# The first stage of a token tower layer rebuilt: other engine orders, split fp32r products, normed rows on ScalarE, a joined row table, gate weights formed later

## The reference, cut to what matters

```python
h = concat(token_table[x], concat(op, var, const, struct, special)[x])     # 128 + 128 columns
# attention, linear, 16 heads of 16, per row of 128 tokens
q, k, v = layernorm(h) @ W_qkv + b_qkv
pq, pk = elu(q) + 1, elu(k) + 1
h = h + pq @ (pk^T v) / (pq . sum(pk) + 1e-6)
# FFN: each token weighs 16 experts
x2 = layernorm(h)
logits = l2norm(x2) @ l2norm(sim) - sigmoid(gates)
rw = softmax over the experts with logits > 0 (the top two, if none is)
q, k, v = sum_e rw_e * (x2 @ {q,k,v}_proj[e]);  causal softmax attention
h = h + sum_e rw_e * (attn @ o_proj[e])
```

## Time and profile before

| | |
|---|---|
| median of 3 runs | 1186.64 us (1185.41 to 1187.48) |
| the profiled execution, own time | 1176.88 us |
| its span, first to last instruction | 1175.0 us |
| busy in the span: PE, DVE, POOL, ACT | 1029.2, 928.9, 754.4, 533.6 us |
| mean granted TensorE clock | 0.973 |

### The profile page before, as it was taken

The page is one execution under the profiler, slowest core; times in us unless marked ns, Lnnn a source line. Parts: engine busy times, 40 slices in busy tenths (PEclk is TensorE's granted clock), DMA queues, the critical chain, the costliest instruction groups (busy, mean ns, idle before and its releaser), DMA issues.

```text
span 1175.0 us, 26735 instructions
## 1 busy us (share of the span) xinstructions
PE 1029.2 (88%) x6571; PEld 862.2 (73%) x6572; DVE 928.9 (79%) x3134; ACT 533.6 (45%) x1455; POOL 754.4 (64%) x975
## 2 busy tenths in 40 slices
PE   1999999999999993599999959999999999999898
PEld 0565656565666662588988849999999889988897
DVE  3789999999999996245544528999888888888898
ACT  3544444444433431234443425555555555555554
POOL 6657777777777756700000037888888888888785
PEclk9999999999999995799999979999999999999999
DMA  5642333333222225576777752333333333333230
GB/s 141 201 151 88 100 104 99 104 95 100 77 86 86 80 75 197 180 231 221 239 223 232 224 177 77 95 91 91 90 90 89 89 89 89 89 89 89 85 93 32
DMA packets 108096, 143.28 MB, mean 122 GB/s; under 512 B 15388, under 2 KB 95330, under 8 KB 107876
## 3 DMA queue, kind: packets, MB, share of 16 engines
q1 hardware_dynamic: 88004, 91.17, 24.4%
q0 software_dynamic: 18880, 50.36, 15.0%
q10 hardware_dynamic: 1152, 1.05, 0.3%
HBM read 77.37 MB, written 72.46 MB: 128 GB/s over the span
## 4 chain that ended last, share of the span: by engine, by line
PE 40%; DVE 22%; POOL 18%; issue 13%; ACT 3%; DMA 2%; POOLq 1%; SPq 0%; DVEq 0%; ACTq 0%
PE bank L1366 8%; PE bank L1291 7%; PE bank L1293 7%; PE bank L1292 7%; PE bank L1298 5%; POOL row_y L747 5%; POOL qk_neg L732 2%; POOL x2T L732 2%; PE bank L1364 2%; DVE phi L1055 2%; POOL x2T L728 2%; POOL x2T L734 2%; POOL qk_neg L728 2%; DVE h L1075 1%; POOL sorted_x L674 1%
## 5 line engine op out<-in xcount | busy, mean ns | idle before, releaser
L1291 PE MATMUL bank<-wo_hi,split_lo 128*128 128x256 f32 x1024 | 302.8, 296 | 4.6 <-DVE qk_e L1228 2.2
L1292 PE MATMUL bank<-wo_lo,split_hi 128*128 128x256 f32 x1024 | 287.3, 281 | 0.0
L1293 PE MATMUL bank<-wo_hi,split_hi 128*128 128x256 f32 x1024 | 287.2, 280 | 0.0
L1291 PEld LDWEIGHTS bank<-wo_hi,split_lo 128*128 128x128 f32 x1024 | 194.5, 190 | 9.3 <-DVE qk_e L1228 4.6
L1366 PE MATMUL bank<-w_attn,x1T 128*128 128x512 f32 (+1 forms) x512 | 201.2, 516 | 0.0
L1292 PEld LDWEIGHTS bank<-wo_lo,split_hi 128*128 128x128 f32 x1024 | 194.5, 190 | 0.0
L1293 PEld LDWEIGHTS bank<-wo_hi,split_hi 128*128 128x128 f32 x1024 | 194.0, 189 | 0.0
L843 ACT ACTIVATE h<-bank,rwo 128x256 f32<-128x256 f32 x256 | 107.4, 471 | 126.8 <-PE bank L1293 99.5
L747 POOL DMA_INDIRECT row_y<-sorted_y,pair_now x128 | 128.4, 1003 | 36.3 <-issue 28.5
L1166 DVE TENSOR_TENSOR split_lo<-bank,split_hi 128x256 fp32r<-128x256 f32 x144 | 61.2, 425 | 104.2 <-ACT split_hi L812 103.0
L740 POOL COPY pair_now<-pair_at 128x2 uint32 (+1 forms) x64 | 13.1, 205 | 195.7 <-SPq L531 195.6
(11 more groups left out here) (223 smaller groups left out, 2516.0 us busy)
## 6 DMA issues: line engine op xcount, KB each, us to landing
sorted_y<-row_y SPq DMA_DIRECT2D x36, 384.0 KB, 3.1
sorted_y<-w_attn SPq DMA_DIRECT2D x36, 384.0 KB, 3.2
row_x<-sorted_x SPq DMA_DIRECT2D x72, 128.0 KB, 2.4
h_rows<-h SPq DMA_DIRECT2D x64, 128.0 KB, 1.8
row_x<-h_rows SPq DMA_DIRECT2D x64, 128.0 KB, 2.9
out_h<-row_x SPq DMA_DIRECT2D x64, 128.0 KB, 2.0
category_table<-in_L_tok_special_table SPq DMA_DIRECT2D x10, 623.0 KB, 5.0
phi<-sorted_x SPq DMA_DIRECT2D x36, 128.0 KB, 2.1
```

The costliest lines, as they stand in the source:

```text
L1291: pe.matmul(ps, left[1][c], right[0][c], start=(c == 0), stop=False)
L1292: pe.matmul(ps, left[0][c], right[1][c], start=False, stop=False)
L1293: last = pe.matmul(ps, left[0][c], right[0][c], start=False, stop=(c == n - 1))
```

## The change: what it does

- **Products.** q, k, v of stage 1 are no longer two fp32 instructions for each half of the contraction but three fp32r ones (hi and lo parts of x1T and of W_qkv). ACT copies x1T to its hi part, DVE subtracts to get the lo part (`x1_lo`, new, every tile). W_qkv is split once, before step 1, into the space of `wo`.
- **Normed rows.** x1 and x2 move from DVE to ACT, as `activation(Identity, scale=root, bias=center)`. DVE makes the new `centers` (-mean times root), one small instruction a step.
- **Roots.** `var_inv` goes; roots_in is two instructions that don't wait for each other. Two small multiplications a group (`energy`) take its place.
- **Gates.** In stage 1 only choosing, counting and placing stay; `weights_formed` goes, and with it the parts of the others that served it. The last 8 tiles are in groups of two. Weights are formed for all 64 tiles in stage 2: a chain of nine small instructions before it, five wide ones (128x1024) in its steps 0 to 4.
- **Joined table.** `embed_table` holds token and category row side by side (1 KB pitch). SP copies both tables into it, ten pieces each of 1250 and 1246 rows of 512 bytes, one of each a step from step -4. From tile 14 on POOL gathers a tile with one indirect DMA, not two.
- **Weights.** Two a step before step 0, and the 16 pieces of `wo` are loaded and split in steps -8 to 7 of stage 2.
- **Orders.** Each engine's order in a step is new. Scatters come as soon as a group is placed; step 1 ends at step 66.

```diff
-    WHOLE_FROM = 14
+    JOINED_FROM = 14
-    GROUPS = B // QUAD
+    GROUPS = [(t, QUAD) for t in range(0, B - 8, QUAD)] + [(t, 2) for t in range(B - 8, B, 2)]
-    N_X2, N_RAW = 11, 4
-    SCATTER_LAG = 7
+    N_X2, N_RAW = 9, 4
+    LAST_STEP = B + 2
...
+        def o_weight_at(i):
+            return 3 * E + i.c + 8 if i.j is None and -8 <= i.c < 8 else None
...   # SP, step 1
+                if 0 <= i.c - COPY_FROM < COPIES:
+                    for skip, at, src in ((N_SMALL, HALF, special_table), (0, 0, token_table)):
+                        n = -(-src.shape[0] // COPIES)
+                        lo, hi = n * (i.c - COPY_FROM), min(n * (i.c - COPY_FROM + 1), src.shape[0])
+                        sp.dma_start(embed[skip + lo:skip + hi, at:at + HALF], src[lo:hi, :]).then_inc(rows_joined, 16)
...   # ACT, step 1, after qk_neg and qk_e of tile i+3
+                    act.activation(x1[:, :], h[t % 8], ACT.Identity, scale=roots[:, t, 0:1],
+                                   bias=centers[:, t, 0:1]).then_inc(done["x1_normed"], 1)
...   # then x2 of tile i+1 in the same way, x1T hi (i+4), pqT (i+3), x2T (i+1), vx (i+3), a weight
...   # DVE, step 1, in order
+   centers(row i+4); phi(i+3); den(i+2); bn_stats of h (i+6); zden(i+2)
+                if x1_tile.inside(B):
+                    after(dve, "x1_T", x1_tile)
+                    dve.tensor_tensor(x1T_s[1], ps_x1[:, 0:C], x1T_s[0].bitcast(F32), ALU.subtract
+                                      ).then_inc(done["x1_lo"], 1)
+   attn, h2, its moments (i+2); roots_in; the gate pieces; kvm(i+3), which waits for kv; a weight
...   # PE, step 1, in order
+   rank product; sums(i+2); turn x1(i+4); logits(i); turn phi(i+3); turn x2(i+1);
+   q and k (i+4), which wait for phi(i+3) and x1_lo(i+4); kv(i+3); v(i+4)
+                for c in range(CH):
+                    for x, w, end in ((1, 0, False), (0, 1, False), (0, 0, c == CH - 1)):
+                        last = pe.matmul(ps[:, 0:hi - lo], turned[x][c], w_attn_s[w][:, c, lo:hi], start=False,
+                                         stop=end)
...   # stage 2: SP, at the head of a step; ACT and DVE, at its end
+                    if o_weight_at(i) is not None:
+                        load_weight(sp, o_weight_at(i))
```

More of the change, by code:

```diff
@@ L408, in run1 @@
         def run1(eng, step):
-            for c in range(-7, B + SCATTER_LAG):
+            for c in range(-7, LAST_STEP + 1):
                 step(Tile(c))
@@ L775, in step1 @@
                     after(act, "qk_negative", tile)
+                    after(act, "phi", tile.shift(-1))
                     act.activation(qk_e[:, :], qk_neg[:, :], ACT.Exp, scale=-1.0).then_inc(done["qk_exp"], 1)
@@ L819, in step2 @@
                                  ).then_inc(done["pair_copied"], 1)
+                    if o_weight_at(i) is not None:
+                        weight_hi(act, o_weight_at(i))
                 run2(act, step2)
             def dense_way():
+                act.wait_ge(weights_v, 2)
+                act.activation(gates_shifted, gates_shifted, ACT.Exp).then_inc(weights_a, 1)
+                for e in range(E):
+                    weight_hi(act, 3 * E + e)
                 def token_tile(t, first):
@@ L1211, in _ @@
             branch(dve, sorted_way, dense_way)
+            dve.wait_ge(routed, 1)
             def add_slot(tile, s):
@@ L1326, in step1 @@
                 if tile.inside(B):
-                    after(pe, "x1_T", tile.shift(-1))
+                    after(pe, "x1_lo", tile.shift(-1))
                     after(pe, "x1_normed", tile)
                     turn(ps_x1, *halves(x1)).then_inc(done["x1_turned"], 1)
+                if i.inside(B):
+                    g = group_of(i.c)
+                    t = i.c - GROUPS[g][0]
+                    if t == 0:
+                        quad_done(pe, "gate_scaled", g - 1)
+                    after(pe, "x2_T", i)
+                    if i.c == 0:
+                        pe.wait_ge(setup_v, 7)
+                    for c in range(CH):
+                        last = pe.matmul(ps_logits[g % 2][:, t, :], halves(x2T)[c], simn[:, c, :],
+                                         start=(c == 0), stop=(c == CH - 1))
+                    last.then_inc(done["logits_product"], 1)
+                tile = i.shift(3)
+                if tile.inside(B):
+                    after(pe, "phi_q_T", tile.shift(-1))
+                    after(pe, "phi", tile)
+                    turn(ps_pq, *halves(phi)).then_inc(done["phi_q_turned"], 1)
                 tile = i.shift(1)
@@ L1334, in step1 @@
                     turn(ps_x2, *halves(x2[tile.c % N_X2])).then_inc(done["x2_turned"], 1)
+                tile = i.shift(4)
+                if tile.inside(B):
+                    after(pe, "phi", tile.shift(-1))
+                    after(pe, "x1_lo", tile)
+                    if tile.c == 0:
+                        pe.wait_ge(setup_v, 6)
+                    attn_product(tile, ps_qk, 0, 2 * C, "qk_product")
                 tile = i.shift(3)
@@ L1337, in step1 @@
                     after(pe, "v_copied", tile)
-                    after(pe, "phi_q_T", tile.shift(-1))
                     after(pe, "kv_masked", tile.shift(-1))
-                    after(pe, "phi", tile)
-                    turn(ps_pq, *halves(phi)).then_inc(done["phi_q_turned"], 1)
                     for g in range(G):
```

507 lines of the change are left out of this document (281 added, 226 removed).

## The result

The changed kernel takes 1202.42 us (median of four runs, 1197.76 to 1205.23) where the kernel before takes 1186.26 beside it: ratio 1.0132, 95% interval 1.0097 to 1.0166. It is slower by 1.3%, where the prediction said 1150 us and faster. Some 12 of them are there because the profiled execution of before is 9.4 us faster than its median and that of the changed kernel 2.8 slower.

A forecast was written before the change was run, and what follows sets the result against it. DVE's instruction chain was taken to bound steps with weights, a PE-ACT-DVE ring those without. Steady steps -50.6, joined table +10, way to stage 2 -5, stage 2's start +9: -36.6, span 1138.4, median 1150 us; range 1122 to 1178.

The forecast's parts named there:

- The joined table: Steps -1 to 5: the 512-byte copies make seven steps 8.0 us instead of 6.5, +10 us.
- Rival (1): Early steps: 512-byte packets cost far more than 30 ns; from 55 ns they eat all the gain; chance 0.08.
- Steady steps: Stage 1, tiles 10 to 63: 5.69 us a step with weights, 5.40 without, gain 50.6 us.
- 5.0 a step: Stage 1: PE's work falls from 6.06 to 5.0 us a step, under DVE's.
- 7 x 0.24: Stage 1, PE: q and k products of a tile take 1.68 us, for 2.33 before.
- the ring that the prediction drew: Stage 1's light step with weights: phi to x1_lo, q and k, kv, kvm, weight split, centers, 4.9 to 5.0 us.
- Rival (3): Stage 1: the new order makes longer waits, each step 6.0 us, 24 us more, 1174; chance 0.13.
- The rival that took the figure of the Trainium skill: Stage 1: ACT copies x1T 0.2 us late each step, 11 us in 53 steps, 1161; chance 0.12.
- x1_lo without wait: Stage 1, DVE: a sign expected in the trace, x1_lo starting without waiting; no size given.
- The way to stage 2: Last q and k product to stage 2's first turn: 37.3 us for 42.2, gain 5.
- about 23: Before stage 2: the fills begin about 23 us after the last product, for 25.6 before.
- Stage 2's start: First sorted tiles: tile 0 is 4 us late and steps 0 to 7 add 5, together +9 us.

The follow-up runs named there:

- later or spread o weights: Changed kernel with o weights loaded and split in steps 8 to 23 of stage 2, 1200.2 us; or loaded every second step, split six steps later, 1197.2 us.
- even copies: Changed kernel with table copies of 1264 and 1248 rows nine times, and what is left the tenth time: 1204.1 us, ratio 1.0234.
- three-edits run: Changed kernel with tables apart again, gathers a step sooner, o weights loaded in steps 4 to 19 of stage 2 and split three steps later: 1191.6 us.

## Why the prediction was wrong

**The joined table (+10; early tiles +29.6, and +4.3 ahead of tile 0).** The price was right, and so were its parts: the queue's 18,413 packets from 40 to 110 us took 46.7% of 16 engines' 70 us, 28.4 ns each, for 30 predicted; the copies ran on 14 and 10 engines; the last 512-byte packet of a step comes 7.9 to 9.0 us after its first copy is issued, for 8.0; and in the order of before the table costs 9.9 us. What failed is that the copies were priced in the old order of a step. The prediction walked the weight and the h2 store behind the copies, but not the third customer of the DMA engines, the gather, whose consumer the same change moved from the end of DVE's step to its middle. Landing up to 5.95 us after its issue instead of 3.2, it holds stats, then x1_lo, then PE, whose clock then drops. Either edit alone, the copies out or the gather sooner, takes 21 us back, and both together all of it (78.8). So 21.3 of the 29.6 go with the copies, with the stall at tile 10 among them; the other 8.3 are the new order without them (87.2 for 78.9), which was in no term. That the lower clock is part of each slow step is read from the products' spacing; no run took it out by itself. Rival (1), which had the right sign, had the wrong mechanism: packets cost 28 ns, not 55. The 4.3 us ahead of tile 0 were in no term; I did not try which of the added set-up steps makes them.

**Steady steps (5.69 and 5.40; 6.30 and 5.99).** DVE's amount was not the bound in any kind of step. In the light step the term that failed is PE's, "5.0 a step": q, k and v take 3.00 us, not 2.52, because "7 x 0.24" and "7 x 0.12" took the bias product for one like the others, and PE's queue is 5.26 without a gap. In the other three the ring that the prediction drew (from phi over x1_lo, q and k, kv and kvm to centers, 4.9) left out the leg that starts at centers: to ScalarE's x1 (0.24), its pass (0.60), the turn, split_hi, x1_lo, 1.84 us in all, with DVE's own 3.7 to 4.7 us from x1_lo to centers in front of it. Rival (3), "longer waits in the new order, each step 6.0", was the right one, and its condition, that x1T is handed around within one step, the right place.

**ScalarE's pass.** The rival that took the figure of the Trainium skill (ScalarE: Activation LUTs, "What ACT_TABLE_LOAD costs": by its formula 585 ns for such a pass) was nearer than the nearest row: the passes took 0.59 and 0.60 us, so the trace agrees. By it the prediction would have had 0.2 us a step more, a third of the 0.6 by which the mean steps are over it. x1 and x2 start 0.51 apart, and in the step shown x1_lo waits 0.22 us for split_hi, so the row "x1_lo without wait" in the list of signs nearly held and said nothing: the lateness sits ahead of it, in ScalarE's 1.0 us wait for centers and DVE's stretch without much to do behind them.

**The way to stage 2 (-5; +2.7).** The fills were last, as predicted, but they didn't begin "about 23" us after the last q and k product. The last placing alone began 23.2 after it (22.0 before the change), and in the eight traces of variants without stalls the fills began 27.2 after it (25.6 before); then they took 6.1 to 6.4 us instead of 7.0. So the way took 40.9 to 41.3 us there: 1 less than before, not 5. The step that failed is that smaller groups and the work taken out would bring the last placing forward; it came 1.2 us later. Why was not taken apart. The other 3.7 us of the profiled execution are the stalls, in SP's 8.4 us from its first read of a fill address to the first fill. DVE's table instructions, which took 10.7 us with theirs for 4.4 before, are not in the chain.

**Stage 2's start (+9; +11.0).** Right in place and in size. Of the 11 us, 4.9 are the time from turn to product (4 predicted), and these the later or spread o weights take back in every trace. 4.0 more lie in sorted tiles 0 to 7 (16.5 us for 12.5; 16.0 to 16.6 in all nine traces with stage 2 unchanged; 16.8 for 12.2 predicted). The rest varies: with stage 2 unchanged, eight traces of the changed order gave 210.5 to 217.5 us, so the profiled 216.8 is at the upper end.

**The sum.** Of the 65 us between the predicted span (1138.4) and 1203.5, tiles 0 to 12 and the start are 26 (29.6 + 4.3 - 10, and 2 of gain priced for tiles 10 and 11), the steady steps 32 (48.8 - 16.6), the way to stage 2 is 8, and stage 2 with the rest nothing (+2.0 - 2.4). The forecast of 1150 has one term more, 9.8 us by which the median stood over the profiled time before the change. Here it stands 2.8 under it, so the medians miss by 52 us and not by 65; that part of the nearness is luck.

## What to carry to other kernels

When a change moves both a transfer and the instruction that waits for some other transfer, price each of them in the new order: the 512-byte copies cost 10 us in one order and some 20 in the other. When copies are cut into pieces, look at the last piece too: the even copies gained 4.5 us in seven steps, and the remainder, on 4 engines, cost it again. Draw the loop from each hand-over back to itself for each kind of step, with the engine that has its queue full on one side and the leg over the others on the other side; 0.33 us of DVE work moved from the one side to beside the leg took 0.35 off the mean step without removing any work. And where a wait leaves PE idle, look at the granted clock of the work behind it: it was paid on top here.

## What the runs showed of the hardware

- Short gaps can cost more than themselves. In the three-edits run PE waited 1.15 us for kvm (until 161.23) and 0.40 for x1 (until 162.32), the granted clock went from 1.00 to 0.50 at 162.5, and it was back at 1.00 at 179.6. The step between with PE busy all the time took 9.87 us, where its neighbours take 5.8 to 6.9.
- Copies within DRAM in 512-byte rows moved 347 GB/s with 1264 and 1248 rows, 307 with 1246, 218 with 1250 and 88 with 1228 and 1124: 22 GB/s for each of 16, 14, 10 and 4 engines. The DMA share is no count of the engines in use: it was 1.15, 1.02, 0.73 and 0.28.
- Engines stalled in some traces and not in others. DVE stood 0.3 to 1.9 us between dependent table instructions, 5.0 to 11.4 us together, and they started again at multiples of about 0.71 us from each other (480.84, 482.27, 484.38, 485.11, 486.51, 487.94); SP took 7.1 to 14.2 us from reading the fill addresses to the first fill, for 3.0 to 3.2 without. All seven traces of the rounds in which before took 1188 us had them, and that of the changed kernel; all eight of those in which it took 1177 had none. The trace of before that is read here had none, and its execution took 1176.9 us where the median beside it was 1186. So part of the 10 us between rounds may lie there; the cause stays open.
